# Another order for the opening of an attention and FP4 feed-forward kernel: maxima in SBUF, shared PSUM banks, no unread products between

## The reference

```python
Q, K, V = xpos(X @ W_Q), xpos(X @ W_K, downscale=True), X @ W_V      # rotary tables, then
p = softmax(Q @ K.T) * D                                             # D = 0.9 ** |n - m|
x = layernorm(X + p @ V)
q4(t): blocks of 16 along the row; scale = max|t| / 6; round t/scale to the FP4 grid; times scale
h = silu(q4(x) @ q4(w_gate).T) * (q4(x) @ q4(w_up).T)                # 704 wide
out = layernorm(x + q4(h) @ q4(w_down).T)
```

## Time and profile before

| | |
|---|---|
| times of three runs | 989.46, 993.35, 994.75 us (median 993.35) |
| profiled execution | 992.2 us, span of its instructions 990.4 us |
| PE busy | 963.4 us, 97% of the span |
| DVE, POOL, ACT busy | 867.0 us (88%), 830.5 us (84%), 648.7 us (65%) |
| TensorE's granted clock | 0.994 of full speed over the span |
| step 3 of the main loop begins on PE | 57.26 us after the span's start |

### The profile page before, as it was taken

One profiled execution on the slowest core, in us unless ns is written; L12 is line 12 of the kernel. 1 busy time (PEld: TensorE's weight loads), 2 busy tenths in 40 slices (PEclk: granted clock), 3 DMA queues, 4 the chain that ended last, 5 costly groups with the idle time before them and its releaser, 6 DMA issues.

```text
span 990.4 us, 20531 instructions
## 1 busy us (share of the span) xinstructions
PE 963.4 (97%) x6002; PEld 872.0 (88%) x6002; DVE 867.0 (88%) x2003; ACT 648.7 (65%) x1575; POOL 830.5 (84%) x1034
## 2 busy tenths in 40 slices
PE   8999999999999999999999999999999999999996
PEld 7788898989998898998989889898899889889886
DVE  6979988988898898898898988898898898989986
ACT  3656667677666667666667666667666667667753
POOL 5988888898889889888889888888888888887763
PEclk9999999999999999999999999999999999999999
DMA  9124235242442425333352423524234242333300
GB/s 315 44 86 128 90 93 171 92 133 88 152 131 70 150 86 171 97 96 118 118 157 92 127 86 96 171 91 126 94 117 150 87 134 81 97 107 108 113 12 23
DMA packets 116112, 111.27 MB, mean 112 GB/s; under 512 B 12576, under 2 KB 93728, under 8 KB 114080
## 3 DMA queue, kind: packets, MB, share of 16 engines
q1 hardware_dynamic: 115312, 108.91, 34.9%
q10 hardware_dynamic: 688, 1.05, 0.3%
HBM read 69.53 MB, written 40.37 MB: 111 GB/s over the span
## 4 chain that ended last, share of the span: by engine, by line
PE 71%; DVE 12%; POOL 6%; issue 4%; DMA 3%; ACT 2%; SPq 1%; DVEq 0%; POOLq 0%; ACTq 0%
PE ps_g L641 10%; PE ps_g L642 9%; PE ps_g L643 9%; PE ps_oy L641 8%; PE ps_oy L643 7%; PE ps_oy L642 7%; PE ps_s L641 4%; PE ps_s L642 4%; PE ps_s L643 4%; PE ps_t L650 3%; DMA landing<-parking 3%; POOL q_l L2506 2%; PE ps_oy L650 1%; POOL h L2483 1%; DVE turned L1870 1%
## 5 line engine op out<-in xcount | busy, mean ns | idle before, releaser
L2483 POOL TENSOR_TENSOR h<-h,hsc 128x704 f32<-128x704 f32 x126 | 168.4, 1337 | 54.5 <-DVE h L1844 38.1
L2598 POOL TENSOR_TENSOR prob<-prob,decay_t 128x512 f32<-128x512 f32 x128 | 164.7, 1297 | 1.9 <-ACT prob L1289 1.9
L641 PE MATMUL ps_oy<-v_h,pt_h 128*128 128x256 f32 x512 | 149.9, 293 | 0.5 <-DVE pt_l L1880 0.4
L641 PE MATMUL ps_g<-wgu_h,xqt_h 128*128 128x480 f32 (+1 forms) x380 | 149.1, 392 | 1.3 <-DVE xqt_l L1899 0.9
L642 PE MATMUL ps_oy<-v_l,pt_h 128*128 128x256 f32 x512 | 145.4, 284 | 0.0
L643 PE MATMUL ps_oy<-v_h,pt_l 128*128 128x256 f32 x512 | 145.3, 284 | 0.0
L643 PE MATMUL ps_g<-wgu_h,xqt_l 128*128 128x480 f32 (+1 forms) x380 | 142.5, 375 | 0.0
L642 PE MATMUL ps_g<-wgu_l,xqt_h 128*128 128x480 f32 (+1 forms) x380 | 142.3, 375 | 0.0
L1801 DVE SCALAR_TENSOR_TENSOR th<-th,ps_g 128x240 f32<-128x240 f32 x188 | 73.5, 394 | 35.2 <-ACT th L1219 32.8
L641 PE MATMUL ps_s<-k_h,q_h 128*128 128x512 f32 x256 | 102.9, 402 | 0.0
L641 PEld LDWEIGHTS ps_oy<-v_h,pt_h 128*128 128x128 f32 x512 | 98.3, 192 | 2.6 <-DVE pt_l L1880 0.8
(11 more groups left out here) (277 smaller groups left out, 3108.4 us busy)
## 6 DMA issues: line engine op xcount, KB each, us to landing
parking<-turned SPq DMA_DIRECT2D x122, 256.0 KB, 2.0
landing<-parking SPq DMA_DIRECT2D x488, 64.0 KB, 2.0
rope_t<-rope SPq DMA_DIRECT2D x15, 1024.0 KB, 5.8
xres<-x SPq DMA_DIRECT2D x64, 128.0 KB, 2.2
out<-yout SPq DMA_DIRECT2D x63, 128.0 KB, 2.0
xin<-x_t SPq DMA_DIRECT2D x14, 512.0 KB, 4.3
first_rope<-rope SPq DMA_DIRECT2D x2, 512.0 KB, 7.7
decay_t<-decay SPq DMA_DIRECT2D x1, 960.0 KB, 12.3
```

Of the source, the lines that this page charges most:

```text
L641: pe.matmul(dst, a_h, b_h, start=(start and i == 0), stop=False)
L2483: return tt(blocks(dst), blocks(src), sc[:, which, at:at + n].unsqueeze(2).to_broadcast([P, n, QB]), ALU.mult)
L2598: tt(prob[:, keys], prob[:, keys], decay_t[:, lo:lo + CW], ALU.mult).then_inc(decayed, 1)
```

## The change

The maxima of weight blocks 0, 1, 3 and 4 move from ps_t to the unused last third of the buffers that hold the block's scales, in SBUF; the instructions that make the scales of these blocks get an accumulator output, whose sum nobody reads. Second V uses ps_g as the first does, one behind the other, and second Q uses ps_t, where the second K was. The weight transposes therefore wait for both V. The unread products between the projections go, the 34 at the start stay. SyncE issues the identity's load ahead of the first gate/up pair instead of behind the second, and ScalarE issues the load of the second X chunk before its first copy. All four lists of the opening are in a new order. The steps of the main loop are not edited.

```diff
@@ constants, semaphores
-WARM_KEYS = (12, 16)
-WARM_VALUES = 5
...
-        first_xh_done = [sem("first_xh_done%d" % c) for c in range(2)]
+        first_xh_done = sem("first_xh_done")
-        first_vh_done = [sem("first_vh_done%d" % c) for c in range(2)]
+        first_vh_done = sem("first_vh_done")
-        unread_done = sem("unread_done")
-        first_vrest_done = [sem("first_vrest_done%d" % c) for c in range(2)]
-        first_vl_done = [sem("first_vl_done%d" % c) for c in range(2)]
+        first_vrest_done = sem("first_vrest_done")
+        first_vl_done = sem("first_vl_done")
@@ banks
-        first_v_bank = (ps_g[:], ps_t_pair)
+        first_v_bank = (ps_g[:], ps_g[:])
@@ w_max
             n = 2 * (CW if m < 3 else FH) // QB
-            return ps_oy[:, 0, 0:n] if m == 2 else ps_t_pair[:, m % 3, 0:n]
+            if m == 2:
+                return ps_oy[:, 0, 0:n]
+            t = w_scale_buffers[m][:]
+            if m == 3:
+                t = t.rearrange("p a n -> p (a n)")
+            return t[:, 2 * n:3 * n]
@@ SyncE's loads
             load_projection(1)
+            sp.dma_start(ident[:], ident_in).then_inc(ident_arrived, 16)
             load_gate_up(0)
...
             load_gate_up(1)
-            sp.dma_start(ident[:], ident_in).then_inc(ident_arrived, 16)
             load_last_gate_up()
@@ weight_transposes, prob_transposes, project_next, rot_mul
                 if g < 2:
-                    pe.wait_ge(first_vl_done[0], 1)
+                    pe.wait_ge(first_vl_done, 2)
                 else:
                     pe.wait_ge(wtl_done, g - 1)
-                if g in (2, 3):
-                    pe.wait_ge(rotmul_done, 2)
...
                 if i == 0:
-                    pe.wait_ge(first_vl_done[1], 1)
+                    pe.wait_ge(first_vl_done, 2)
+                    pe.wait_ge(rotmul_done, 2)
...
-                project(which, ps_g, (xt_h, xt_l), k_done if which else q_done)
+                project(which, ps_t_pair if c == 1 else ps_g, (xt_h, xt_l), k_done if which else q_done)
...
-                tt((rot_a, rot_b)[i][:], ps_g[:], tab, ALU.mult).then_inc(rotmul_done, 1)
+                tt((rot_a, rot_b)[i][:], ps_t_pair if c == 1 else ps_g[:], tab, ALU.mult).then_inc(rotmul_done, 1)
@@ TensorE's list
             project(0, first_bank[1], first_xt[0], first_p_done[1])
-            unread_products(ps_t_pair[:, 1, 0:D], WARM_KEYS[0]).then_inc(unread_done, 1)
-            pe.wait_ge(first_mul_done[0], 2)
-            unread_products(ps_g[:, 0, 0:D], WARM_KEYS[1])
             pe.wait_ge(first_xl_done[1], 1)
-            pe.wait_ge(wscale_done, 2)
             project(1, first_bank[2], first_xt[1], first_p_done[2])
             pe.wait_ge(wqkvl_done, 3)
             pe.wait_ge(first_mul_done[0], 2)
             first_values(0)
+            first_values_rest(0)
+            pe.wait_ge(first_vl_done, 1)
+            first_values(1)
             pe.wait_ge(first_rot_done[1], 2)
-            unread_products(ps_s[:, 0, 0:D], WARM_VALUES)
-            first_values_rest(0)
-            unread_products(ps_s[:, 0, 0:D], WARM_VALUES)
+            scores(0, 0)
+            first_values_rest(1)
+            scores(0, 1)
             pe.wait_ge(ident_arrived, 16)
             weight_transposes(0)
-            scores(0, 0)
+            pe.wait_ge(first_rot_done[2], 2)
+            project_next(0, 1)
             weight_transposes(1)
-            pe.wait_ge(first_rot_done[2], 2)
-            pe.wait_ge(wscale_done, BLOCKS)
-            first_values(1)
-            scores(0, 1)
-            first_values_rest(1)
-            pe.wait_ge(wtl_done, 2)
-            project_next(0, 1)
             scores(1, 0)
             scores(1, 1)
+            prob_transposes(0, 0)
             weight_transposes(2)
+            prob_transposes(0, 1)
+            scores(2, 0)
             weight_transposes(3)
-            prob_transposes(0, 0)
-            prob_transposes(0, 1)
             weight_transposes(4)
+            scores(2, 1)
+            values_product_first(0)
             weight_transposes(5)
-            values_product_first(0)
+            weight_transposes(6)
+            prob_transposes(1, 0)
+            weight_transposes(7)
+            prob_transposes(1, 1)
+            weight_transposes(8)
             values_product_second(0)
-            weight_transposes(6)
-            scores(2, 0)
-            weight_transposes(7)
-            weight_transposes(8)
-            scores(2, 1)
-            prob_transposes(1, 0)
-            prob_transposes(1, 1)
@@ ScalarE's list
+            act.dma_start(first_x[1], x_chunks[1]).then_inc(first_x_arrived[1], 16)
             first_x_high(0)
-            act.dma_start(first_x[1], x_chunks[1]).then_inc(first_x_arrived[1], 16)
             first_weight_high(0)
             first_weight_high(1)
             first_x_high(1)
+            first_weight_high(2)
             weight_magnitude(0)
-            first_weight_high(2)
...
@@ VectorE: weight_max, weight_scales
-                if m >= 3:
-                    dve.wait_ge(first_rot_done[2], 2)
...
-                if m == 1:
-                    dve.wait_ge(unread_done, 1)
...
-                nc.vector.tensor_scalar(w_scale(m, 1), w_max(m), TIES_DOWN / 6.0, MIN_SCALE, ALU.mult, ALU.max)
+                sums = [None if m == 2 else xsc[:, 0, 2 * m + n:2 * m + n + 1] for n in range(2)]
+                nc.vector.tensor_scalar(w_scale(m, 1), w_max(m), TIES_DOWN / 6.0, MIN_SCALE, ALU.mult, ALU.max,
+                                        accum_out=sums[0])
...
-                                        ALU.mult, ALU.max).then_inc(wscale_done, 1)
+                                        ALU.mult, ALU.max, accum_out=sums[1]).then_inc(wscale_done, 1)
@@ VectorE's list
             first_multiply(0, 0)
+            weight_max(1)
             first_multiply(0, 1)
             first_multiply(1, 0)
-            weight_max(1)
             first_weight_low(2)
+            weight_scales(1)
             first_multiply(1, 1)
-            weight_scales(1)
+            weight_reciprocals(1)
             first_turn(1, 0)
+            first_multiply(2, 0)
             weight_shift(0)
             first_turn(1, 1)
+            first_multiply(2, 1)
             weight_grid(0)
...
@@ GpSimd's list
             nc.gpsimd.memset(mhalf[:], -0.5).then_inc(mhalf_set, 1)
+            first_x_low()
             weight_units(0)
             first_turn(0)
-            first_x_low()
             first_turn(1)
             first_rotated_low(0, 0)
+            weight_units(1)
...
```

More of the change, by code:

```diff
@@ L678, in first_values_rest @@
                 pe.wait_ge(minus_ident_set, 1)
-                pe.wait_ge(first_vh_done[c], 1)
+                pe.wait_ge(first_vh_done, c + 1)
                 at = half_of(0) * (NT * D) + c * 4 * D
@@ L697, in first_keys @@
                 pe.wait_ge(wqkvh_done, 1)
-                pe.wait_ge(first_xh_done[0], 1)
+                pe.wait_ge(first_xh_done, 1)
                 for m in range(2):
@@ L1136, in first_x_high @@
                 act.wait_ge(first_x_arrived[c], 32 if c == 0 else 16)
-                nc.scalar.copy(first_xt[c][0], first_x[c]).then_inc(first_xh_done[c], 1)
+                nc.scalar.copy(first_xt[c][0], first_x[c]).then_inc(first_xh_done, 1)
             def first_rotated_high(r, a):
@@ L1406, in _ @@
             weight_high(7)
+            probs_high(1, 0)
             weight_high(8)
+            exponential(2)
             r1_mean(0)
-            probs_high(1, 0)
             r1_squares(0)
             probs_high(1, 1)
-            exponential(2)
             first_norm(0)
@@ L2035, in _ @@
             weight_reciprocals(2)
+            weight_scales(3)
             weight_max(4)
-            weight_scales(3)
+            weight_reciprocals(3)
             weight_shift(1)
@@ L2040, in _ @@
             weight_grid(1)
+            weight_reciprocals(4)
+            row_max(0)
+            weight_shift(2)
+            rot_mul(0, 1, 0)
             weight_low(0)
-            weight_reciprocals(3)
-            weight_low(1)
-            weight_shift(2)
-            weight_reciprocals(4)
+            rot_mul(0, 1, 1)
             weight_grid(2)
-            row_max(0)
+            row_max(1)
             weight_shift(3)
             weight_grid(3)
-            rot_mul(0, 1, 0)
-            rot_mul(0, 1, 1)
+            weight_low(1)
+            weight_low(2)
             weight_shift(4)
             weight_grid(4)
-            weight_low(2)
+            probs_low(0, 0)
             weight_low(3)
-            probs_low(0, 0)
+            weight_low(4)
+            row_max(2)
+            weight_low(5)
             probs_low(0, 1)
-            row_max(1)
-            weight_low(4)
-            weight_low(5)
+            weight_low(6)
+            weight_low(7)
             row_inverse(0)
-            weight_low(6)
+            weight_low(8)
             first_residual(0)
-            weight_low(7)
```

(8 more changed lines are left out.)

56 lines of the change are left out of this document (25 added, 31 removed).

## The result

The changed kernel takes 996.13 us (median of 11 runs, 991.27 to 998.18), the kernel before, on the same chip, 992.73 us (11 runs, 988.67 to 994.75). The ratio is 1.0042, with an interval of 1.0027 to 1.0057: slower, by less than the 0.5% that count as a change here. The profiled execution took 998.18 us, its span 996.3 us: 5.9 us more than the one of before. It is the slowest of the 11; the medians lie 3.4 us apart. The forecast was 993.4 us, the range 989.7 to 997.0.

What follows compares the result with a forecast made beforehand. DVE was taken to bound the opening; 2.3 + 0.8 + 1.1 - 0.4 us on 34.5 of work, with remaining waits, left step 3 at 57.1. Change 0.0 +- 1.5 us: 993.4 us forecast, range 989.7 to 997.0.

Steps and rivals of the forecast that it cites:

- The opening's end: End of DVE's opening list: weight_low(8) near 54.2 us against 53.85, step 3 on PE at 57.1 against 57.26.
- The stall in front of `weight_max(1)`: DVE in the opening: idle about 2.2 us, from 12.1, until the second gate/up pair lands near 14.3.
- rival B: Closing waits go too and the second gate/up pair lands by 13.0: step 3 near 54.5, 990.6 us; chance 0.20.
- the step that decides: DVE's new list: weight_max(1) between the first K's two multiplies, waiting for the second gate/up pair, about 2.2 us idle.
- X earlier: ScalarE's X load in the opening, issued near 1.7 us: lands near 9.6 instead of 12.5, second K from 13.3.
- PE's own waits: PE in the opening: 2.8 us at 16.0, 1.3 and 1.4 around the first V's rest, 2.0 near 41.7, covered by DVE.
- Accumulators: Accumulator outputs of four blocks' scales on DVE: two reads of 0.1 us each, 0.8 us in all, could be 0.65.
- Rival D: Scales reading SBUF stand behind POOL's instructions, 0.8 us each, 3.2 us in all: 996.6 us; chance 0.05.
- rows 6: Profile rows of the steady state's scales: 156 ns plus an accumulator read of 82 ns.
- Rival C: Low clock from 26.7 us on costs 2.1 us, another fall behind the wait at 41.7 costs 1.1: 996.6 us; chance 0.17.
- stretches after step 3 that differ by over 2 us: Main loop: sign that the forecast is wrong, meaning the opening's order reaches further than its end.
- The 38 unread products: Products removed from PE's opening, 5.2 us of PE: nothing counted, since PE is not the chain's engine there.

Runs made afterwards that it cites:

- e8: Changed kernel with the second block's maxima moved back behind the two multiplies of the first K; ratio 1.0014 to the kernel before.
- e5: Changed kernel with 38 unread products put back around the first V and its rest (76 instructions more); ratio 0.9996 to the kernel before.
- e10: Changed kernel with the second block's maxima moved back, table reload first in steps j = 1 and 5, and 30 unread products; 983.63 us, ratio 0.9908 to before.
- e11: Changed kernel without the accumulator outputs of the scales of blocks 0, 1, 3 and 4; ratio 1.0085 to the kernel before.
- e7: Changed kernel with 17 opening products of 512 columns in place of 34 of 256 (34 instructions fewer); ratio 1.0004 to the kernel before.
- e1: Changed kernel with 72 opening products of 120 columns in place of 34 of 256 (76 instructions more); ratio 1.0090 to the kernel before.
- e2: Kernel before with its unread products twice as wide and half as many (70 instructions fewer), orders unchanged; ratio 1.0047 to the kernel before.
- e3: Changed kernel with the 1 MB table reload issued first in steps j = 1 and 5, ahead of the parks; 985.77 us, ratio 0.9951 to before.
- e4: Kernel before with the 1 MB table reload issued first in steps j = 1 and 5, ahead of the parks; 984.55 us, ratio 0.9934.
- e6: Changed kernel with 72 opening products of 16 weight and 120 moving columns for 34 of 128 and 256 (76 instructions more); ratio 1.0007 to before.

## Why the prediction was right and wrong

- *The opening's end.* Forecast: `weight_low(8)` ends near 54.2, step 3 on PE at 57.1. Measured 54.4 and 57.34. Right, but in part by luck: the stall came out 0.65 us shorter than forecast and the accumulators' 0.8 us were not there, while a fall of the clock that the sum did not have cost 1.1 to 1.2 (below). The errors cancelled.
- *The stall in front of `weight_max(1)`.* Forecast 2.2 us, ended at 14.3 by the second gate/up pair. Measured 1.55 us, ended at 13.98 by that load. Right in kind; e8 priced the step at up to 2.2 us at step 3, of which about 1.1 us are the place itself by e5 and e10. That is what rival B gave for an earlier landing. It was "the step that decides", as the prediction said, together with the clock that went with it.
- *X earlier.* Forecast to land at 9.6. It landed by 8.0: ScalarE's copy of it starts at 8.03, GpSimd's low half at 9.15, and the second K began at 12.77 (forecast 13.3). The estimate by shares of the queues was 1.6 us too slow; nothing hung on it.
- *PE's own waits.* Forecast 2.8, 1.3, 1.4, 2.0; measured 2.63, 1.19, 1.16, 1.91.
- *Accumulators.* Forecast 0.8 us, with 0.65 as the floor. Measured: scales follow each other every 0.14 us with the read and every 0.13 without (18.60, 18.73, 18.86 in the kernel before), so the read lies under the next instruction. The term is near 0.1 us for all eight (an estimate from that difference); worse, the sign of the edit was not seen: without it step 3 comes 2.8 us later (e11). Rival D, which *rows 6* spoke against, is the true mechanism of a plain scale in SBUF; those rows are of the accumulator form and could not speak on the plain one.
- *The clock.* Rival C's second fall came, at 26.1, where it was to cost 2.1 us, and the third, behind the wait before 44.15, did not. Step 3 stayed where it was laid out. But e5 and e7, without the second fall, began it 1.1 to 1.2 us earlier than the new kernel (-1.10 and -0.93 for +0.13): about half of C's 2.1 us was paid, and other terms of the sum made it good.
- *The step that failed* is the premise of the argument: that nothing after the opening is edited, "so its whole effect is how much earlier or later step 3 of the main loop begins". The traced execution lost 5.75 us in the loop (3.3 by the medians) and 0.13 in the opening, and the prediction's own mark for that ("stretches after step 3 that differ by over 2 us") was hit. The 38 unread products, for which it counts nothing, were not free: e1, e2 and e5 to e7 indicate that their number, not their columns, moves the loop. 996.13 us lies inside the stated range all the same, but in the part that was there for rivals C and D, and neither of them made the loss: that is luck.

What is shown: with no order changed, fewer instructions of TensorE made the kernel before 0.47% slower (e2, 0.29 to 0.65%); and the reload's place on the queue is worth 0.7 to 0.9% (e3, e4), through waits at the turned probabilities and the low clock behind them. e1 and e5 to e7 point the same way for the new kernel, but the new kernel itself was not timed beside them, and it and e7 are not clearly apart in the loop. What was only read from traces: that the packet of the fetch lengthens the reload and SP's issue. For the issue the traces leave little room (110 of 110); for the reload six of six at that distance speak for it, and others of over 7 us without it show that something else does it too. No run moved a fetch and nothing else. The state that the new order of the opening might leave behind is not excluded as a smaller part. Open as well: single runs of the new kernel reach from 991.27 to 998.18 us at granted clocks from 0.998 to 0.989, so the waits or the falls behind them are not the same in every execution.

## What to carry to other kernels

A change of the opening can move the time of a loop that it does not touch: when stretches far behind an edit differ, compare the DMA queues there, and look whether a bulk load stands ahead of a small one that an engine awaits; moving that load 9 us ahead was worth 0.7 and 0.9% (e4 against before; e3 against the new kernel, by their two ratios), where the whole change cost 0.4%. One trace is one execution: before a stretch of it is explained, see where its time lies among the others of the same kernel. Before a product or a wait is removed from a tuned kernel because it costs nothing, try the kernel with as many instructions as before. A row excludes a cost only for its own form of instruction: the scale with an accumulator said nothing about the scale without.

## What the runs showed of the hardware

- What reads as a fetch of TensorE's program is a packet of 16 KB every 256 instructions on average. Every issue of a DMA by SP that took over 1.0 us (110 of 9,889; the median is 0.43) overlaps such a packet. Of 63 reloads of 1 MB in the j = 5 steps, the six with the packet 3 us behind their issue took 7.06 to 7.56 us, the others 5.2 to 6.8 but for two of e11 (7.37 and 8.80).
- In the loop the granted clock fell to 0.5 for 3.4 us at waits of 1.80 (e2), 1.82 (before), 2.12 (e6), 2.18 and 2.24 (new) and 2.60 us (e1), and did not at waits of 1.98 (e5), 2.00 (e6), 2.02 (e11) and 2.19 us (e8).
- At the low clock a product of 120 columns with 128 weight columns comes every 0.21 us (e1), one of 256 columns too (new kernel, 0.12 at full clock), one of 120 columns with 16 weight columns every 0.10 (e6, 0.06 at full clock).
- A plain `tensor_scalar` of 128 x 44 in SBUF took up to 1.98 us beside a GpSimd instruction of 1.94 us, and 0.13 to 0.19 with an accumulator output.
